# Attention step 0: first half of each tile with one wide exponential, the shift by the maximum and the sums on VectorE

## The chip, the cores and the metric

The kernel runs on one core of one Trainium2 chip. The metric is the device time of one execution in microseconds, the median of several.

## The reference, cut to what matters

A decoder block with post layer norm on x of shape (8, 512, 512), in float32:

```python
x = layernorm(x + mixing(x))               # per head: cumulative sum of FFT products, then w_out
x = layernorm(x + cross_attention(x, ctx)) # 16 heads of 32, 77 keys
x = layernorm(x + ffn(x))                  # weight rounded to int4 levels, bias, low-rank part

def cross_attention(q, c, mask):
    q, k, v = q @ W_q + b_q, c @ W_k + b_k, c @ W_v + b_v      # 16 heads
    scores = einsum('bhqd,bhkd->bhqk', q, k) / sqrt(32)
    scores = where(mask == 0, -1e6, scores)
    attn = softmax(scores, axis=-1)
    return einsum('bhqk,bhkd->bhqd', attn, v) @ W_o + b_o
```

The change touches the softmax of the first of the eight batches.

## The kernel before, in words

Three programs follow one another: `prepare` (weights, keys and values), `mix_tokens` (the mixing of all eight batches) and `attend` (cross attention and the last linear layer). Every float32 matmul is made of three: the operands are split into a high part, a rounded copy made by ScalarE, and a low part, the remainder, made by VectorE.

`attend` runs over steps. Step i holds the scores and the softmax of batch i, the turning of x1 and the projection of q of batch i + 1, and the weighing of values, the output projection and the last layer of batch i - 1. Step 0 has no batch behind it, so it has only the first two. Steps 1 to 6 share one order, steps 7 and 8 have their own.

A batch has 512 tokens, four tiles t of 128. The scores of a tile, 16 heads by 77 keys, are 1232 numbers in each partition. They lie in `score_ps`, four PSUM banks with four heads each, and one tile's scores fill it. Half h is two banks, eight heads, 616 scores. For each tile and half:

- TensorE: `score(i, t, h)`, six matmuls of 308 columns. It waits until the exponentials of the same half of the tile before have read `score_ps` (semaphore `exped`).
- VectorE: `softmax_top(i, t, h)`, which writes the masked value (`copy_predicated`, L1658) and takes the negated maximum of each head (L1663) into `top` (`topped`).
- ScalarE: `exponentials(i, t, h)`, eight instructions (L1352), one a head, with the negated maximum as bias and the sum taken by the accumulator. They write `probs`, which has room for two tiles.
- VectorE: `invert_totals(i, t)`, one reciprocal of the 16 sums (L1670).
- GpSimd: `normalize_probs(i, t, h)`, two multiplications of 616 (L1501).
- TensorE: `turn_probs(i, t, c)`, three groups of four transposes (L1146), named P{t}{c}. ScalarE copies each group (L1359) and VectorE takes its remainder (`split_probs`, L1642), which frees the bank.

Beside this TensorE turns the next batch's x1 (`turn_x1`, L1109, X0 to X3, split by L1335 and L1615) and projects q (`project_q`, Q0 to Q3, twelve matmuls of 512 columns, split by L1340 and L1623).

The P, X and Q groups share four PSUM banks, `shared_ps`, in the fixed order `START_ORDER`: P00 P01 P02 X0 X1 X2 X3 P10 P11 P12 Q0 P20 P21 Q1 P22 Q2 P30 P31 P32 Q3. Each use waits until the use four places before it has been emptied by VectorE (semaphore `freed`, counted in this order).

Every engine has its own list of calls, written out by hand. Its instructions run in that order, each held only by semaphores. Late in step 0 ScalarE also splits the two weights `w_o` and `w_ffn` (L1439, L1445), VectorE takes the remainder of `w_o` (L1825), and GpSimd that of `w_ffn`.

Of the kernel before, what the change touches and what calls it, by code (L numbers as in the profile page):

```python
# [21 lines left out]
ALU = mybir.AluOpType  # L22
ACT = mybir.ActivationFunctionType
AX = mybir.AxisListType

P = 128
B, S, D = 8, 512, 512
NT = S // P
# [3 lines left out]
XH, XHD = 16, 32  # L32
# [22 lines left out]
def wait_reuse(eng, sem, value):  # L55

    if not isinstance(value, int) or value > 0:
        eng.wait_ge(sem, value)
# [900 lines left out]
def attend(nc, ins, out, x1_dram, k_dram, v_dram, ffn_dram, ident, half_power, w_q, bias_q, bias_v, bias_o, bias_f,  # L959
# [3 lines left out]
    with ExitStack() as ctx:  # L963
# [35 lines left out]
        turned, turned_hi = sem("turned_p"), sem("pT_hi_ready")  # L999
        stat_done, stat_seen, aggr_done = sem("stat_done"), sem("stat_seen"), sem("aggr_done")  # L1000
# [101 lines left out]
        def _(pe):  # L1102
# [20 lines left out]
            def score(i, s, t, h):  # L1123

                if t == 0:

                    pe.wait_ge(k_loaded, nth(i, 1, 0) * (16 * 2 * GH))
                    pe.wait_ge(q_hi, nth(i, NC, 2 * h + 1))
                    pe.wait_ge(freed, s.emptied_before(f"Q{2 * h + 1}"))

                wait_reuse(pe, exped, i * (NT * XH) + ((t - 1) * XH + (h + 1) * XH // 2))
                tok = slice(t * P, (t + 1) * P)
                for g in (2 * h, 2 * h + 1):
                    last = split_matmuls(nc, score_ps[:, g, 0:GK],
                                         [([q[:, g, tok] for q in qT], [k[:, g, :] for k in k_block])])
                last.then_inc(scored, 1)
# [115 lines left out]
            turn_x1(1, s, 0)  # L1252
            score(0, s, 2, 1)
            turn_x1(1, s, 1)
            score(0, s, 3, 0)
# [4 lines left out]
            turn_probs(0, s, 1, 2)  # L1260
            score(0, s, 3, 1)
# [69 lines left out]
        def _(act):  # L1331
# [10 lines left out]

            def exponentials(i, t, h):

                act.wait_ge(topped, nth(i, NT * 2, 2 * t + h))
                if h == 0:

                    wait_reuse(act, turned, i * NT * 3 + (3 * (t - 1)))
                    wait_reuse(act, totalled, i * NT + (t - 1))
                for j in range(h * XH // 2, (h + 1) * XH // 2):  # L1350
                    g, k = j // GH, j % GH
                    nc.scalar.activation(probs[:, t % 2, j * KEYS:(j + 1) * KEYS],  # L1352
                                         score_ps[:, g, k * KEYS:(k + 1) * KEYS], ACT.Exp, bias=top[:, t % 2, j:j + 1],
                                         accum_out=total[:, t % 2, j:j + 1]).then_inc(exped, 1)
# [60 lines left out]
            exponentials(0, 0, 0)  # L1415
            exponentials(0, 0, 1)
            exponentials(0, 1, 0)
            exponentials(0, 1, 1)
            exponentials(0, 2, 0)
            split_probs(0, s, 0, 0)  # L1420
            split_probs(0, s, 0, 1)
            split_probs(0, s, 0, 2)
            split_x1(1, s, 0)
            exponentials(0, 2, 1)
            split_x1(1, s, 1)
# [5 lines left out]
            exponentials(0, 3, 0)  # L1431
# [177 lines left out]
        def _(dve):  # L1609
# [55 lines left out]

            def invert_totals(i, t):
# [122 lines left out]
            softmax_top(0, 0, 0)  # L1789
            softmax_top(0, 0, 1)  # L1790
            softmax_top(0, 1, 0)
            invert_totals(0, 0)
            softmax_top(0, 1, 1)
            softmax_top(0, 2, 0)
            invert_totals(0, 1)
            softmax_top(0, 2, 1)
            split_probs(0, s, 0, 0)
            split_probs(0, s, 0, 1)
            split_probs(0, s, 0, 2)
            split_x1(1, s, 0)  # L1800
            softmax_top(0, 3, 0)
            invert_totals(0, 2)
            split_x1(1, s, 1)
            split_x1(1, s, 2)
            split_x1(1, s, 3)
            softmax_top(0, 3, 1)
            split_probs(0, s, 1, 0)
            split_probs(0, s, 1, 1)
            split_probs(0, s, 1, 2)
            find_hidden(1)  # L1810
            invert_totals(0, 3)
            split_q(1, s, 0)
# [8 lines left out]

# [172 lines left out]
```

## Time and profile before

| | |
|---|---|
| median of three runs | 968.82 us |
| lowest and highest run | 965.21 and 971.74 us |
| profiled execution, first to last instruction (the page gives no other time for it) | 964.6 us |
| TensorE busy in it | 917.6 us |
| VectorE busy | 666.7 us |
| ScalarE busy | 376.8 us |
| GpSimd busy | 337.8 us |
| mean granted clock of TensorE | 0.982 |

Busy time is the union of an engine's instructions. Waiting on semaphores is not busy. The granted clock is the share of TensorE's full clock that it was given.

### The profile page before, as it was taken

The numbers are of one execution on the slowest core, as the hardware profiler recorded it, in microseconds if no ns is written. First come the engines' busy times: TensorE is split into PE (matmuls) and PEld (weight loads), VectorE is DVE, ScalarE is ACT, GpSimd is POOL, SyncE is SP. The second block draws the span as 40 slices with busy tenths as digits, with TensorE's granted clock in tenths as the row PEclk, the third lists the DMA queues.
The fourth block names the chain that finished last, engine by engine and source line by source line (L and its number), as shares of the span: only waits on it lengthen the run. The fifth ranks groups of instructions, "written<-read, shape, count | busy, mean of one in ns | idle before, by whom it ended". The sixth has DMA issues, their size and how long they took to land.

```text
span 964.6 us, 14638 instructions
## 1 busy us (share of the span) xinstructions
PE 917.6 (95%) x4476; PEld 754.5 (78%) x4476; DVE 666.7 (69%) x1128; ACT 376.8 (39%) x1403; POOL 337.8 (35%) x310
## 2 busy tenths in 40 slices
PE   5898999999999999999779999999999999999987
PEld 4784888888888888888668788888888888888775
DVE  3363466665656565555667888979889798887957
ACT  3152120101010111102287566656567565666610
POOL 2000243232222232324236434444443444433733
PEclk9998999999999999999979999999999999999999
DMA  5944201221203020203423122131222203120021
GB/s 179 326 148 172 90 1 52 80 80 52 104 28 127 3 87 1 88 23 116 134 81 102 25 79 73 40 113 24 89 63 78 75 21 122 30 89 21 17 77 44
DMA packets 72346, 76.02 MB, mean 79 GB/s; under 512 B 38567, under 2 KB 40871, under 8 KB 72303
## 3 DMA queue, kind: packets, MB, share of 16 engines
q1 hardware_dynamic: 72303, 75.49, 24.4%
q8 instruction: 22, 0.36, 0.2%
q14 instruction: 21, 0.17, 0.1%
HBM read 52.60 MB, written 22.87 MB: 78 GB/s over the span
## 4 chain that ended last, share of the span: by engine, by line
PE 41%; DVE 4%; ACT 2%; issue 2%; POOL 2%; POOLq 0%; DVEq 0%
PE shared_ps L74 31%; PE score_ps L74 4%; PE shared_ps L1146 4%; ACT probs L1352 2%; PE shared_ps L1109 1%; PE shared_ps L1179 1%; POOL probs L1501 1%; DVE score_ps L1658 1%; DVE xT_lo L1615 0%; DVE x_and_res L1704 0%; DVE top_s L1663 0%; DVE pT_lo L1642 0%; POOL x_and_res L1516 0%; DVE y L1682 0%; DVE w_o_lo L1825 0%
## 5 line engine op out<-in xcount | busy, mean ns | idle before, releaser
L1352 ACT ACTIVATE probs<-score_ps,top_s 128x77 f32<-128x77 f32 x512 | 159.0, 359 | 36.9 <-DVE top_s L1663 36.9
L1352 ACT ACTIVATION_READ_ACCUMULATOR probs<-score_ps,top_s 128x1 f32 x512 | 122.9, 240 | 0.0
L1501 POOL TENSOR_TENSOR probs<-probs,per_total 128x616 f32<-128x616 f32 x64 | 82.7, 1309 | 65.9 <-DVE per_total L1670 65.7
L1494 POOL TENSOR_TENSOR rstd<-ve,half_power 128x1 f32<-128x1 f32 x64 | 42.4, 662 | 157.1 <-DVE ve L1693 152.5
L722 POOL TENSOR_TENSOR vals<-qs_prod 128x512 f32<-128x512 f32 x32 | 41.1, 1296 | 127.1 <-DVE qs_prod L804 127.1
L713 POOL TENSOR_TENSOR mix_rstd<-mix_ve,half_power 128x1 f32<-128x1 f32 x32 | 22.0, 688 | 175.4 <-DVE mix_ve L823 175.4
L1658 DVE COPY_PREDICATED score_ps<-hidden,masked 128x616 f32<-128x616 int32 x64 | 66.2, 1034 | 11.6 <-PE score_ps L74 11.6
L1359 ACT ACTIVATE pT_hi<-shared_ps 103x512 fp32r<-103x512 f32 (+1 forms) x96 | 54.7, 612 | 46.0 <-PE shared_ps L1146 45.5
L672 ACT ACTIVATE v_sb<-v_ps 128x512 f32<-128x512 f32 x32 | 18.9, 594 | 133.9 <-PE v_ps L74 133.9
L679 ACT ACTIVATE qT_hi<-vals 128x512 fp32r<-128x512 f32 x32 | 19.4, 631 | 122.3 <-POOL vals L722 106.2
L1642 DVE TENSOR_TENSOR pT_lo<-shared_ps,pT_hi 103x512 fp32r<-103x512 f32 (+1 forms) x96 | 64.5, 684 | 0.0
L1146 PE MATMUL shared_ps<-ident,probs 128*103 128x128 f32 (+1 forms) x384 | 53.9, 279 | 2.6 <-POOL probs L1501 1.8
L74 PE MATMUL shared_ps<-w_o_hi,xT_hi 128*128 128x512 f32 x128 | 53.3, 417 | 2.3 <-DVE xT_lo L1623 1.9
L74 PE MATMUL shared_ps<-w_ffn_hi,xT_hi 128*128 128x512 f32 x120 | 50.1, 418 | 5.5 <-DVE xT_lo L1615 4.9
L1516 POOL TENSOR_TENSOR x_and_res<-x_and_res,bias_f 128x512 f32<-128x512 f32 x32 | 42.2, 1318 | 35.9 <-DVE x_and_res L1704 23.1
L1146 PEld LDWEIGHTS shared_ps<-ident,probs 128*103 128x103 f32 (+1 forms) x384 | 47.0, 158 | 9.7 <-POOL probs L1501 2.7
L1663 DVE TENSOR_REDUCE top_s<-score_ps 128x8 f32<-128x616 f32 x64 | 51.2, 800 | 3.6
L815 DVE TENSOR_TENSOR mix_r<-out_ps,x_res 128x512 f32<-128x512 f32 x29 | 20.1, 692 | 47.3 <-PE out_ps L74 47.3
L74 PE MATMUL v_ps<-xT_hi,w_spec_hi 128*128 128x512 f32 x128 | 50.6, 395 | 1.9 <-DVE xT_lo L766 1.9
L74 PE MATMUL k_ps<-xT_hi,w_spec_hi 128*128 128x512 f32 x128 | 51.7, 404 | 0.0
L74 PE MATMUL q_ps<-xT_hi,w_spec_hi 128*128 128x512 f32 x128 | 51.2, 400 | 0.0
L74 PE MATMUL shared_ps<-w_o_hi,xT_lo 128*128 128x512 f32 x128 | 50.7, 396 | 0.0
(218 smaller groups left out, 2660.1 us busy)
## 6 DMA issues: line engine op xcount, KB each, us to landing
x_tok<-in_x SPq DMA_DIRECT2D x8, 1024.0 KB, 5.9
x_res<-in_x SPq DMA_DIRECT2D x8, 1024.0 KB, 8.0
x_between<-mix_x SPq DMA_DIRECT2D x32, 256.0 KB, 2.0
x<-x_between SPq DMA_DIRECT2D x8, 1024.0 KB, 5.5
x_tok<-x_between SPq DMA_DIRECT2D x8, 1024.0 KB, 5.7
out<-y_out SPq DMA_DIRECT2D x32, 256.0 KB, 2.0
wqkv_sb<-in_w_qkv SPq DMA_DIRECT2D x4, 768.0 KB, 7.8
keys_split<-w_q_hi SPq DMA_DIRECT2D x8, 154.0 KB, 5.4
```

The source lines that it names most:

```text
L74: last = nc.tensor.matmul(out, l, r, start=(n == 0), stop=(n == len(terms) - 1))
L713: nc.gpsimd.tensor_tensor(rstd[:, t % 2:t % 2 + 1], ve[:, t % 2:t % 2 + 1], half_power[:], ALU.pow).then_inc(rstd_ready, 1)
L722: nc.gpsimd.tensor_tensor(vals[:, h, :], qs[:, 2 * h, :], qs[:, 2 * h + 1, :], ALU.subtract if h else ALU.add).then_inc(vals_summed, 1)
L1146: last = nc.tensor.transpose(shared_ps[s.bank(use)][0:size, g * P:(g + 1) * P], probs[:, t % 2, g * GK + at:g * GK + at + size], ident[:])
L1352: nc.scalar.activation(probs[:, t % 2, j * KEYS:(j + 1) * KEYS], score_ps[:, g, k * KEYS:(k + 1) * KEYS], ACT.Exp, bias=top[:, t % 2, j:j ...
L1359: nc.scalar.activation(pT[0][0:size, c, :, t * P:(t + 1) * P], turned_bank(s, t, c), ACT.Copy).then_inc(turned_hi, 1)
L1494: nc.gpsimd.tensor_tensor(rstd[:, n:n + 1], ve[:, n:n + 1], half_power[:], ALU.pow).then_inc(rstd_ready, 1)
L1501: nc.gpsimd.tensor_tensor(p, p, per_total[:, t % 2, h * heads:(h + 1) * heads].unsqueeze(2) .to_broadcast([P, heads, KEYS]), ALU.mult).the ...
L1516: nc.gpsimd.tensor_tensor(res2[:, t % 2, :], x2[:, t % 2, :], bias_f[:], ALU.add).then_inc(res2_ready, 1)
L1642: nc.vector.tensor_tensor(pT[1][0:size, c, :, tok], turned_bank(s, t, c), pT[0][0:size, c, :, tok].bitcast(F32), ALU.subtract).then_inc(fr ...
L1658: nc.vector.copy_predicated(s4, hidden[:, t, :].unsqueeze(1).unsqueeze(1).to_broadcast(shape), masked[:].unsqueeze(1).unsqueeze(1).to_broa ...
L1663: nc.vector.tensor_reduce(top[:, t % 2, h * 8:(h + 1) * 8].rearrange("p (g j) -> p g j", j=GH), s4, AX.X, ALU.max, negate=True).then_inc(t ...
```

## The change

It touches step 0 alone. For the first half of each tile, `exponentials(0, t, 0)` becomes `wide_exponential(t)`: one instruction over the 616 scores in `probs`, in place. VectorE's new `shift(t)` first adds the negated maxima to the scores and writes them to `probs`, and its new `sum_probs(t)` adds up the exponentials of each head. Two semaphores are new. TensorE's scores of the first half of the next tile wait for `shifted` and no longer for the exponentials. The second half keeps its eight exponentials.

The orders of step 0 are changed on three engines. On TensorE X1 comes ahead of score (2, 1), and score (3, 0) moves from ahead of X2 to behind P12. On ScalarE the first half of tile 2 comes behind the copies of P00 to P02, and X1's copy ahead of the second half of tile 2. On VectorE the remainders of P00 to P02 come ahead of both halves of tile 2, those of X0 and X1 ahead of the second half of tile 2, those of X2, X3 and P10 to P12 ahead of tile 3, and each inversion stands behind a sum.

```diff
--- before.py
+++ after.py
@@ -997,6 +997,7 @@
         scored, hid, topped, exped, totalled, normed = (sem("scored"), sem("hid"), sem("topped"), sem("exped"),
                                                        sem("per_total_ready"), sem("normed"))
         turned, turned_hi = sem("turned_p"), sem("pT_hi_ready")
+        shifted, summed = sem("shifted"), sem("summed")
         stat_done, stat_seen, aggr_done = sem("stat_done"), sem("stat_seen"), sem("aggr_done")
         var_eps, rstd_ready, x2_ready, y_ready = sem("var_eps_b"), sem("rstd_b"), sem("x2_ready"), sem("y_ready")
         y_stored = [sem(f"y_stored{n}") for n in range(2)]
@@ -1128,7 +1129,10 @@
                     pe.wait_ge(q_hi, nth(i, NC, 2 * h + 1))
                     pe.wait_ge(freed, s.emptied_before(f"Q{2 * h + 1}"))
 
-                wait_reuse(pe, exped, i * (NT * XH) + ((t - 1) * XH + (h + 1) * XH // 2))
+                if isinstance(i, int) and i == 0 and h == 0:
+                    wait_reuse(pe, shifted, t)
+                else:
+                    wait_reuse(pe, exped, i * (NT * XH) + ((t - 1) * XH + (h + 1) * XH // 2))
                 tok = slice(t * P, (t + 1) * P)
                 for g in (2 * h, 2 * h + 1):
                     last = split_matmuls(nc, score_ps[:, g, 0:GK],
@@ -1250,14 +1254,14 @@
             turn_probs(0, s, 0, 1)
             turn_probs(0, s, 0, 2)
             turn_x1(1, s, 0)
+            turn_x1(1, s, 1)
             score(0, s, 2, 1)
-            turn_x1(1, s, 1)
-            score(0, s, 3, 0)
             turn_x1(1, s, 2)
             turn_x1(1, s, 3)
             turn_probs(0, s, 1, 0)
             turn_probs(0, s, 1, 1)
             turn_probs(0, s, 1, 2)
+            score(0, s, 3, 0)
             score(0, s, 3, 1)
             project_q(1, s, 0)
             turn_probs(0, s, 2, 0)
@@ -1340,10 +1344,15 @@
                 nc.scalar.activation(qT[0][:, c, :], shared_ps[s.bank(use)][:], ACT.Identity,
                                      bias=bias_q[:, c:c + 1]).then_inc(q_hi, 1)
 
+            def wide_exponential(t):
+                act.wait_ge(shifted, t + 1)
+                half = probs[:, t % 2, 0:XH // 2 * KEYS]
+                nc.scalar.activation(half, half, ACT.Exp).then_inc(exped, XH // 2)
+
             def exponentials(i, t, h):
 
                 act.wait_ge(topped, nth(i, NT * 2, 2 * t + h))
-                if h == 0:
+                if h == 0 or (isinstance(i, int) and i == 0):
 
                     wait_reuse(act, turned, i * NT * 3 + (3 * (t - 1)))
                     wait_reuse(act, totalled, i * NT + (t - 1))
@@ -1412,23 +1421,23 @@
 
 
             s = Shared(0, False, True, True)
-            exponentials(0, 0, 0)
+            wide_exponential(0)
             exponentials(0, 0, 1)
-            exponentials(0, 1, 0)
+            wide_exponential(1)
             exponentials(0, 1, 1)
-            exponentials(0, 2, 0)
             split_probs(0, s, 0, 0)
             split_probs(0, s, 0, 1)
             split_probs(0, s, 0, 2)
+            wide_exponential(2)
             split_x1(1, s, 0)
+            split_x1(1, s, 1)
             exponentials(0, 2, 1)
-            split_x1(1, s, 1)
             split_x1(1, s, 2)
             split_x1(1, s, 3)
             split_probs(0, s, 1, 0)
             split_probs(0, s, 1, 1)
             split_probs(0, s, 1, 2)
-            exponentials(0, 3, 0)
+            wide_exponential(3)
             exponentials(0, 3, 1)
             split_q(1, s, 0)
             split_probs(0, s, 2, 0)
@@ -1662,6 +1671,25 @@
                 wait_reuse(dve, exped, i * NT * XH + (t - 1) * XH)
                 nc.vector.tensor_reduce(top[:, t % 2, h * 8:(h + 1) * 8].rearrange("p (g j) -> p g j", j=GH), s4, AX.X,
                                         ALU.max, negate=True).then_inc(topped, 1)
+
+            def shift(t):
+
+                dve.wait_ge(topped, 2 * t + 1)
+                wait_reuse(dve, turned, 3 * (t - 1))
+                shape = [P, GROUPS // 2, GH, KEYS]
+                s4 = score_ps[:, 0:2, 0:GK].rearrange("p g (j k) -> p g j k", j=GH)
+                low = top[:, t % 2, 0:XH // 2].rearrange("p (g j) -> p g j", j=GH).unsqueeze(3).to_broadcast(shape)
+                nc.vector.tensor_tensor(probs[:, t % 2, 0:XH // 2 * KEYS].rearrange("p (g j k) -> p g j k", j=GH, k=KEYS),
+                                        s4, low, ALU.add).then_inc(shifted, 1)
+
+            def sum_probs(t):
+
+                dve.wait_ge(exped, t * XH + XH // 2)
+                wait_reuse(dve, totalled, t - 1)
+                nc.vector.tensor_reduce(total[:, t % 2, 0:XH // 2],
+                                        probs[:, t % 2, 0:XH // 2 * KEYS].rearrange("p (j k) -> p j k", k=KEYS), AX.X,
+                                        ALU.add).then_inc(summed, 1)
+                dve.wait_ge(summed, t + 1)
 
             def invert_totals(i, t):
                 dve.wait_ge(exped, nth(i, NT * XH, t * XH + XH - 1))
@@ -1787,29 +1815,37 @@
             find_hidden(0)
             s = Shared(0, False, True, True)
             softmax_top(0, 0, 0)
+            shift(0)
             softmax_top(0, 0, 1)
             softmax_top(0, 1, 0)
+            shift(1)
+            sum_probs(0)
             invert_totals(0, 0)
             softmax_top(0, 1, 1)
-            softmax_top(0, 2, 0)
-            invert_totals(0, 1)
-            softmax_top(0, 2, 1)
             split_probs(0, s, 0, 0)
             split_probs(0, s, 0, 1)
             split_probs(0, s, 0, 2)
+            softmax_top(0, 2, 0)
+            shift(2)
+            sum_probs(1)
+            invert_totals(0, 1)
             split_x1(1, s, 0)
-            softmax_top(0, 3, 0)
-            invert_totals(0, 2)
             split_x1(1, s, 1)
+            softmax_top(0, 2, 1)
             split_x1(1, s, 2)
             split_x1(1, s, 3)
-            softmax_top(0, 3, 1)
             split_probs(0, s, 1, 0)
             split_probs(0, s, 1, 1)
             split_probs(0, s, 1, 2)
+            softmax_top(0, 3, 0)
+            shift(3)
+            sum_probs(2)
+            invert_totals(0, 2)
+            softmax_top(0, 3, 1)
             find_hidden(1)
+            split_q(1, s, 0)
+            sum_probs(3)
             invert_totals(0, 3)
-            split_q(1, s, 0)
             split_probs(0, s, 2, 0)
             split_probs(0, s, 2, 1)
             split_q(1, s, 1)
@@ -1818,7 +1854,6 @@
             split_probs(0, s, 3, 0)
             split_probs(0, s, 3, 1)
             split_probs(0, s, 3, 2)
-
             dve.wait_ge(w_hi, 1)
             dve.wait_ge(w_loaded[0], 16)
             for c in range(NC):
```

## Rows read from the trace of the kernel before

**Rows 1.** The page's first part: busy time, share of the span, instructions.

```profile
PE 917.6 (95%) x4476; PEld 754.5 (78%) x4476; DVE 666.7 (69%) x1128; ACT 376.8 (39%) x1403; POOL 337.8 (35%) x310
```

**Rows 2.** By stage: length, busy PE, PEld, DVE, ACT, POOL, clock, DMA, GB/s.

```profile
475.00:518.10 43.10, 33.42 (x162) 29.01 (x163) 28.32 (x46) 33.74 (x149) 13.58 (x11) 0.80 0.30 92
518.10:964.60 446.50, 430.14 (x2240) 360.82 (x2238) 371.15 (x665) 250.04 (x1093) 207.14 (x188) 0.99 0.22 63
```

**Rows 3.** Waits in step 0: who for whom, us in total, times, longest.

```profile
POOL probs L1501 <- DVE per_total L1670: 22.6, 4, 7.0
...
PE score_ps L74 <- ACT probs L1352: 5.5, 3, 2.9
```

**Rows 4.** TensorE's timeline in step 0: start, duration, tile, idle before.

```profile
481.83 0.41 PE L74 MATMUL score_ps<-xT_hi,qT_hi 128*128 128x308 f32 x1 [2.93 <-ACT probs L1352]
...
484.29 0.62 PE L74 MATMUL score_ps<-xT_hi,qT_hi 128*128 128x308 f32 x1 [1.08 <-ACT probs L1352]
...
487.68 0.63 PE L74 MATMUL score_ps<-xT_hi,qT_hi 128*128 128x308 f32 x1 [1.48 <-ACT probs L1352]
...
489.38 2.76 PE L1146 MATMUL shared_ps<-ident,probs 128*103 128x128 f32 x12
491.94 1.00 PE L1109 MATMUL shared_ps<-ident,x 128*128 128x128 f32 x4
...
496.25 1.11 PE L1109 MATMUL shared_ps<-ident,x 128*128 128x128 f32 x4 [2.47 <-DVE pT_lo L1642]
...
503.42 0.40 PE L74 MATMUL shared_ps<-xT_hi,w_q_hi 128*128 128x512 f32 x1
...
506.17 1.17 PE L1146 MATMUL shared_ps<-ident,probs 128*103 128x128 f32 x8
...
515.05 0.50 PE L74 MATMUL shared_ps<-xT_hi,w_q_hi 128*128 128x512 f32 x1 [0.26 <-DVE qT_lo L1623]
...
517.91 0.30 PE L74 MATMUL score_ps<-xT_hi,qT_hi 128*128 128x308 f32 x1
```

**Rows 5.** VectorE's timeline in step 0, same columns.

```profile
483.38 0.81 DVE L1658 COPY_PREDICATED score_ps<-hidden,masked 128x616 f32<-128x616 int32 x1 [2.65 <-PE score_ps L74]
484.23 0.80 DVE L1663 TENSOR_REDUCE top_s<-score_ps 128x8 f32<-128x616 f32 x1
484.94 0.24 DVE L1670 RECIPROCAL per_total<-total 128x16 f32<-128x16 f32 x1
486.38 0.81 DVE L1658 COPY_PREDICATED score_ps<-hidden,masked 128x616 f32<-128x616 int32 x1 [1.19 <-PE score_ps L74]
...
491.32 0.24 DVE L1670 RECIPROCAL per_total<-total 128x16 f32<-128x16 f32 x1
...
495.51 1.88 DVE L1642 TENSOR_TENSOR pT_lo<-shared_ps,pT_hi 103x512 fp32r<-103x512 f32 x3
...
500.65 0.24 DVE L1670 RECIPROCAL per_total<-total 128x16 f32<-128x16 f32 x1
```

**Rows 6.** ScalarE's timeline in step 0: first and ninth exponential, two copies.

```profile
479.22 0.33 ACT L1352 ACTIVATE probs<-score_ps,top_s 128x77 f32<-128x77 f32 x1 [4.90 <-DVE top_s L1663]
...
481.63 0.37 ACT L1352 ACTIVATE probs<-score_ps,top_s 128x77 f32<-128x77 f32 x1
...
500.74 0.60 ACT L1359 ACTIVATE pT_hi<-shared_ps 103x512 fp32r<-103x512 f32 x1
...
511.38 1.91 ACT L1439 ACTIVATE w_o_hi<-x_tok 128x2048 fp32r<-128x2048 f32 x1
```

**Rows 7.** VectorE's timeline in step 1: a mask.

```profile
529.47 3.75 DVE L1658 COPY_PREDICATED score_ps<-hidden,masked 128x616 f32<-128x616 int32 x1
```

**Rows 8.** GpSimd's timeline beside that mask.

```profile
530.17 2.39 POOL L1501 TENSOR_TENSOR probs<-probs,per_total 128x616 f32<-128x616 f32 x2
```

**Rows 9.** TensorE's timeline in step 1, after a wait.

```profile
543.43 0.47 PE L74 MATMUL shared_ps<-w_ffn_hi,xT_hi 128*128 128x512 f32 x1 [2.33 <-DVE xT_lo L1615]
...
547.85 1.03 PE L1146 MATMUL shared_ps<-ident,probs 128*103 128x128 f32 x8
```

## The prediction

> **What bounds the kernel now.** I read the page's busy times first. TensorE is busy 95% of the span and VectorE 69% [rows 1]. Cut by stage, the 43.1 us of attention step 0 stand out: TensorE is busy 33.4 of them, so some 9.7 us are idle, and its mean granted clock is 0.80 against 0.99 in the 446.5 us behind, in which it is busy for 430 us [rows 2]. The steps behind are bound by TensorE. So what counts is when TensorE's first score of step 1 starts, now at 517.91 [rows 4].
>
> The waits in step 0 say for whom it idles: two long ones before the scores of tile 1 and one before those of tile 2, for ScalarE's exponentials, 5.5 us in all [rows 3]; and 2.47 us before the second turn of x1, which needs the bank of a P piece that VectorE has not yet emptied [rows 4]. GpSimd waits 22.6 us for the inverted sums [rows 3]. That costs nothing now: the turns of tile 1's P start at about 500, and its sums are inverted at 491.32, those of tile 2 at 500.65 for turns at 506.17 [rows 4, 5]. The order written for VectorE keeps these slacks, and this is what the change touches.
>
> **The prices.** A mask with its maximum takes 1.56 us until VectorE's next instruction (483.38 to 484.94), and others see the maximum 0.83 after the reduction starts [rows 5]. Eight exponentials with their accumulator reads take 2.41 us (479.22 to 481.63) [rows 6]. The shift over 616 elements isn't in the trace. The nearest row is the reduction over the same 616 scores from PSUM, 0.80 us, 0.71 until the next instruction [rows 5]; three subtractions of 512 take 1.88, about 0.6 each [rows 5], so the ends are 0.6 and, if a broadcast operand ran at the mask's pace, 0.81. I take 0.72, and 0.83 for whoever depends on it. The same for the sum over 616 of SBUF, and 0.1 more before the inversion, which waits for it. The wide exponential lies between the copies of 512 (0.60) and 2048 elements (1.91): 0.85 ns an element, so 0.69 us, with 0.6 until the next [rows 6]; the low end is 0.60, the high end, if an exponential carried the 0.1 that 77-element ones (0.33) have over that line at its start, 0.79.
> A score of six matmuls takes 2.1 us until its mask starts (484.29 to 486.38) [rows 4, 5] at half clock, 1.2 of 2.4 GHz; at full clock some 0.7 less, half of the time that its matmuls take. Twelve turns of P take 2.56 at half clock (489.38 to 491.94) [rows 4]. A projection of q is 2.75 (503.42 to 506.17) [rows 4].
>
> **What is gained.** In each of four tiles ScalarE gives back 2.41 - 0.60 = 1.8 us, 7.2 in all. TensorE's scores of the next tile's first half wait for a shift and not for eight exponentials.
> Tile 0: mask at 477.5, shift at 479.2, seen at 480.05. Tile 1's first scores start there, not at 481.83 [rows 4]: 1.8 us early. But the second maximum of tile 0 now stands behind the shift and comes at 481.6; its eight exponentials run 481.6 to 484.05; before the change the ninth began at 481.63 [rows 6], and they ended at 484.03. Nothing is gained there. The second half of tile 1 waits for them: 484.15, against 484.29 [rows 4]. Its eight exponentials end at 490.4 as before.
> Tile 2's first scores follow at once, at 485.9 (before: 487.68 [rows 4]), and the first turn of P waits for GpSimd instead: shift, sum and inversion of tile 1 and 0 stand in VectorE's queue, so tile 0 is inverted at 485.4 (before 484.94 [rows 5]), normalized in 3 us to 488.7, turned from 488.8 (before 489.38 [rows 4]). X0, X1, score 2/1, X2 and X3 then run without a wait, since VectorE now empties the banks from 491.0 and not from 495.51 [rows 5]. TensorE is through with them at 495.2; before, they ended at about 500. Up to here the change is 4.8 us ahead, and the 2.47 us wait is gone.
>
> **What is lost.** VectorE now does the three remainders of tile 0's P (491.0 to 493.1) ahead of the mask of tile 2. Then mask and maximum (to 494.8), shift (495.5), sum of tile 1 (496.2), inversion at 496.3. Before it was 491.32 [rows 5]: 5.0 us later. GpSimd normalizes from 496.7 in 2.39 [rows 8] and tile 1 can be turned at 499.2. TensorE, done at 495.2, waits 4.0 us: the lead is lost to the first new wait, on tile 1's sums.
> Beside it, ScalarE's wide exponential of tile 2 waits for its shift until 495.6, and ahead of x1's copies, which end at 497.2. VectorE's remainders of X0 and X1 are ahead of mask 2/1: 498.1, maximum 499.7, exponentials to 502.1, only then X2's copy and remainder, 503.4. The last turn of tile 1 needs X2's bank: 503.5, a second wait, 2.5 us. Behind it come score 3/0 (504.5), 3/1 and the first projection of q, at 507.6 in half clock, at 505.7 in full; before, 503.42 [rows 4].
> Tile 3's first mask waits for score 3/0: 506.5. Maximum, shift and the sum of tile 2 follow, and tile 2 is inverted at 509.7, against 500.65 [rows 5]: 9 us later. Normalized at 512.4, turned at 512.6, against 506.17 [rows 4]: 6.4 us late, a third wait of 2.2 us behind the first projection. Tile 3's sum waits for nothing that matters: inverted at 516.2, normalized at 518.9, turned from 521.4.
>
> **The clock.** After the wait of 2.33 us in step 1 the twelve matmuls of 512 columns take 4.42 us (543.43 to 547.85), where 2.75 is the rate at full clock [rows 4, 9]: 1.7 us more. The third new wait meets the same work, two turns and a projection, so I add 1.7. From 512.6: turns and Q1 to 518.2, P22 and Q2 to 521.4, tile 3's turns to 522.7, 0.4 more for Q2's bank, and the last projection at 523.1. It was at 515.05 [rows 4]: 8.1 us late. Walking the old order with the same prices puts it at 515.6, 0.6 too late, so I take 7.5.
>
> **What follows the stage.** The splitting of w_o and w_ffn, the last q's and bias additions all hang on the same late events and move along. TensorE has 16 us idle in the 446.5 behind [rows 2], spread and at the end, so little can be made up. Sum: +7.5 us. No transfer is moved. The profiled execution would go from 964.6 to 972.1. The page gives only its span; the median of the three runs is 4.2 us above it, and they spread by 6.5. So 968.8 + 7.5 = 976.3.
>
> **The rivals.**
> *The shorter chain pays through.* If VectorE's queue did not hold back the second halves and sums, two exponential groups on the way to tile 2 would shrink from 2.41 to 0.72: 3.4 us, 965.4, faster than before. For it: exponentials are what TensorE waits for now [rows 3]. It decides at the turns of tile 1: it holds if they start before 496. Against it: their sums stand behind seven VectorE instructions, of which the first wait for ScalarE's copies. 6%.
> *Clock or step 1 gives back.* At full clock all through the walk ends 4.9 us late; or the 2.33 us wait of step 1, with its 1.7 of slow clock, closes in a shifted order, 7.5 - 4.0 = 3.5. About 973. 20%.
> *Collisions on top.* A mask in step 1 took 3.75 us where 0.81 is usual: it lasted until GpSimd had finished two multiplications, 530.17 to 532.56 [rows 5, 7, 8]. Now mask 2/1 (498.1) falls into GpSimd's work on tile 1 (496.7 to 499.1), on the path: up to 1 us. Mask 3/1 meets tile 2's: 0.6 to 2.4. With half clock held longer behind the third wait, 1 to 2 more: 3 in the middle, up to 6, so 979 to 982, over 1% slower. 25%.
> The Trainium skill, SBUF — State Buffer, "Who interferes with whom", says that a VectorE instruction with two SBUF inputs and a GpSimd one that reads SBUF hold the shared pair exclusively, and whoever starts first blocks the other. By that rule mask 2/1 waits whole, as the row of 529.47 shows; without it this rival would lose most of its chance.
> *It does not do what it says:* shift or sum at twice the price. Two shifts and two sums on the path: up to +3 beside the above; or everything is hidden, 0. 4%.
> The forecast itself, +5.5 to +9.5: 45%.
>
> **How the numbers follow.** Likeliest: 976.3. 1% is 9.7 us, about what a measurement can tell. Over it lie most of the collisions and an edge of the forecast with the scatter of medians: 0.27. Faster by over 1% needs three times the rival's gain: 0.03. Range: from just above the first rival, 967, to the heavy end with 2 us of scatter, 984.
>
> **What would show it.** Tile 1's first scores near 480.1; no wait before X1; TensorE idle 4 us before tile 1's turns, released by GpSimd, 2.5 before its last turn, released by VectorE's X2, and about 2 before tile 2's, by GpSimd; inversions near 485.4, 496.3, 509.7 and 516.2; step 1's first score near 525.5. Wrong is the prediction if tile 2 is inverted before 505, if TensorE never waits for GpSimd, or if the end moves otherwise than step 1's start.

## The result, and the profile after

The median went from 967.13 us (965.21 to 971.74, four runs) to 975.99 us (974.07 to 978.69, four runs), 8.9 us more: a ratio of 1.0093, 95% interval 1.0058 to 1.0127. The median of before that the prediction had in hand, 968.82, was that of three of these runs.

The profiled executions differ by more, 964.6 against 975.9 us. 1.8 us of this had arisen before step 0: its first score starts at 477.38 and not at 475.58, in code that is the same. In all the profiles of this study, of kernels that are the same up to there, it starts between 474.7 and 477.9. So times within step 0 are given below less 1.8, or from the first score on.

TensorE's timeline of the changed kernel, with the idle time before an instruction and its releaser in brackets:

```profile
477.38 0.38 PE L74 MATMUL score_ps<-xT_hi,qT_hi 128*128 128x308 f32 x1 [1.99 <-PEq L457]
...
482.73 0.41 PE L74 MATMUL score_ps<-xT_hi,qT_hi 128*128 128x308 f32 x1 [3.42 <-DVE probs L1682]
...
486.87 0.62 PE L74 MATMUL score_ps<-xT_hi,qT_hi 128*128 128x308 f32 x1 [2.67 <-ACT probs L1361]
...
490.92 1.56 PE L1150 MATMUL shared_ps<-ident,probs 128*103 128x128 f32 x12 [0.65 <-POOL probs L1510]
...
494.50 0.66 PE L1110 MATMUL shared_ps<-ident,x 128*128 128x128 f32 x4 [1.58 <-DVE pT_lo L1651]
...
501.53 2.03 PE L1150 MATMUL shared_ps<-ident,probs 128*103 128x128 f32 x8 [4.65 <-POOL probs L1510]
506.83 1.09 PE L1150 MATMUL shared_ps<-ident,probs 128*102 128x128 f32 x4 [3.27 <-DVE xT_lo L1624]
...
510.71 0.40 PE L74 MATMUL shared_ps<-xT_hi,w_q_hi 128*128 128x512 f32 x1
...
516.18 1.12 PE L1150 MATMUL shared_ps<-ident,probs 128*103 128x128 f32 x8 [2.57 <-POOL probs L1510]
517.06 0.48 PE L74 MATMUL shared_ps<-xT_hi,w_q_hi 128*128 128x512 f32 x1
...
521.48 0.60 PE L1150 MATMUL shared_ps<-ident,probs 128*102 128x128 f32 x4
...
529.27 0.30 PE L74 MATMUL score_ps<-xT_hi,qT_hi 128*128 128x308 f32 x1
```

Compare with [rows 4]. From the first score of step 0 to that of step 1 it is 51.9 us, where it was 42.3: 9.6 more. Behind it are 446.6 and 446.7 us, so nothing was given back and nothing lost. Three waits are new or have grown: 4.65 us before the turns of tile 1, released by GpSimd, 3.27 before its last turn, released by VectorE's remainders of x1 (0.89 at this place before), and 2.57 before the turns of tile 2, by GpSimd again. The projection behind the third runs at half clock for most of its length: 517.06 to 521.48, 4.42 us.

VectorE's timeline, the lines that answer to [rows 5] and the new ones:

```profile
477.44 2.62 DVE L1658 TENSOR_SCALAR hidden<-mask 128x308 int32<-128x308 int32 x1
480.19 0.81 DVE L1667 COPY_PREDICATED score_ps<-hidden,masked 128x616 f32<-128x616 int32 x1
...
481.87 0.80 DVE L1682 TENSOR_TENSOR probs<-score_ps,top_s 128x616 f32<-128x616 f32 x1
...
486.77 0.78 DVE L1689 TENSOR_REDUCE total<-probs 128x8 f32<-128x616 f32 x1
487.58 0.25 DVE L1698 RECIPROCAL per_total<-total 128x16 f32<-128x16 f32 x1
...
498.75 0.25 DVE L1698 RECIPROCAL per_total<-total 128x16 f32<-128x16 f32 x1
...
500.55 1.59 DVE L1667 COPY_PREDICATED score_ps<-hidden,masked 128x616 f32<-128x616 int32 x1
...
512.86 0.25 DVE L1698 RECIPROCAL per_total<-total 128x16 f32<-128x16 f32 x1
...
519.34 0.25 DVE L1698 RECIPROCAL per_total<-total 128x16 f32<-128x16 f32 x1
```

The shift takes 0.80 us and the sum 0.78. The second inversion is at 498.75 and the third at 512.86, against 491.32 and 500.65 [rows 5]. The mask at 500.55 lasts 1.59 us, and the table of hidden keys at 477.44 lasts 2.62. The wide exponential on ScalarE:

```profile
482.76 0.72 ACT L1350 ACTIVATE probs<-probs 128x616 f32<-128x616 f32 x1 [6.64 <-DVE probs L1682]
```

GpSimd's normalization of tiles 1 and 2:

```profile
499.09 2.39 POOL L1510 TENSOR_TENSOR probs<-probs,per_total 128x616 f32<-128x616 f32 x2 [8.22 <-DVE per_total L1698]
513.19 2.94 POOL L1510 TENSOR_TENSOR probs<-probs,per_total 128x616 f32<-128x616 f32 x2 [11.71 <-DVE per_total L1698]
```

The waits of step 0, for whom, in total, times, longest:

```profile
POOL probs L1510 <- DVE per_total L1698: 31.5, 4, 11.7
...
PE shared_ps L1150 <- POOL probs L1510: 7.9, 3, 4.6
```

GpSimd waits 31.5 us for the inverted sums, where it was 22.6 [rows 3], and TensorE now waits 7.9 us for GpSimd, where it did not wait at all. The 5.5 us for the exponentials of [rows 3] have become 3.42 for the first shift and 2.67 for exponentials.

Event by event, the changed kernel's times less 1.8:

| event | before | forecast | measured |
|---|---|---|---|
| first scores of tile 1 | 481.83 | 480.05 | 480.9 |
| tile 0 inverted | 484.94 | 485.4 | 485.8 |
| turns of tile 0 | 489.38 | 488.8 | 489.1 |
| tile 1 inverted | 491.32 | 496.3 | 496.9 |
| turns of tile 1 | about 500 | 499.2 | 499.7 |
| last turn of tile 1 | | 503.5 | 505.0 |
| first projection | 503.42 | 507.6 | 508.9 |
| tile 2 inverted | 500.65 | 509.7 | 511.1 |
| turns of tile 2 | 506.17 | 512.6 | 514.4 |
| last projection | 515.05 | 523.1 | 524.6 |
| first score of step 1 | 517.91 | 525.5 | 527.5 |

### The profile page after: what moved, and what is told of

The parts are those of the page before. It is cut to its first block, busy times and chain, and to the rows that moved or that the text cites. A ratio compares the mean times of both kernels' runs of the same rounds, so it can differ in the third digit from the quotient of the medians.

```text
span 975.9 us, 14596 instructions
## 1 busy us (share of the span) xinstructions
PE 918.2 (94%) x4476; PEld 754.6 (77%) x4476; DVE 675.0 (69%) x1136; ACT 368.9 (38%) x1343; POOL 337.8 (35%) x310
## 3 DMA queue, kind: packets, MB, share of 16 engines
q1 hardware_dynamic: 72303, 75.49, 24.2%
## 4 chain that ended last, share of the span: by engine, by line
PE 40%; DVE 4%; issue 3%; ACT 2%; POOL 2%; POOLq 0%; DVEq 0%; ACTq 0%
PE shared_ps L74 30%; PE score_ps L74 4%; PE shared_ps L1150 3%; ACT probs L1361 2%; POOL probs L1510 1%; DVE score_ps L1667 1%; PE shared_ps L1110 1%; PE shared_ps L1183 1%; DVE top_s L1672 1%; DVE xT_lo L1624 0%; DVE x_and_res L1732 0%; DVE pT_lo L1651 0%; DVE hidden L1658 0%; POOL x_and_res L1525 0%; DVE y L1710 0%
## 5 line engine op out<-in xcount | busy, mean ns | idle before, releaser
L1361 ACT ACTIVATE probs<-score_ps,top_s 128x77 f32<-128x77 f32 x480 | 148.9, 356 | 38.1 <-DVE top_s L1672 38.1
L1361 ACT ACTIVATION_READ_ACCUMULATOR probs<-score_ps,top_s 128x1 f32 x480 | 114.6, 239 | 0.0
L74 PE MATMUL v_ps<-xT_hi,w_spec_lo 128*128 128x512 f32 x128 | 51.3, 401 | 0.0
L74 PE MATMUL v_ps<-xT_lo,w_spec_hi 128*128 128x512 f32 x128 | 51.2, 400 | 0.0
```

What stands on the lines that cost most here:

```text
L74: last = nc.tensor.matmul(out, l, r, start=(n == 0), stop=(n == len(terms) - 1))
```

## The experiments

The theory: the orders cost the time, not the added arithmetic. The sums of tiles 1 and 2 stand behind remainders that wait for others, and X2's bank hangs on the late second half of tile 2. The main rival: VectorE's eight added instructions, four shifts and four sums. Each kernel is compared with runs of the kernel before on the same chip, whose medians were 966.2 to 966.8 us. "Stage" is the time from the first score of step 0 to the first value matmul of step 1 in the profiled execution: 43.2 us before, 52.7 in the changed kernel. "Rest" is what follows: 445.9 and 445.8. Both are of one execution each. A projection can run at half clock in one and at full clock in another at the same place, which is worth 1.6 us (the rows are below, under the remainder of w_o and under the clearings), so a smaller difference of stage or rest is no finding by itself.

### The two halves of the change apart

`o1_orders_alone` has the changed kernel's orders and the arithmetic of before. Against the changed kernel, for each tile like this:

```diff
-            wide_exponential(0)
+            exponentials(0, 0, 0)
...
             softmax_top(0, 0, 0)
-            shift(0)
...
-            sum_probs(0)
             invert_totals(0, 0)
```

`a1_arith_alone` has the changed kernel's arithmetic in the orders of before: each shift right behind its half's maximum and each sum right ahead of its inversion, but for the shift of tile 3. Against the kernel before, on VectorE:

```diff
             softmax_top(0, 3, 0)
+            sum_probs(2)
             invert_totals(0, 2)
             split_x1(1, s, 1)
             split_x1(1, s, 2)
             split_x1(1, s, 3)
+            shift(3)
             softmax_top(0, 3, 1)
```

> The arithmetic of before (eight exponentials with accumulators in the first half too, no shift, no sum), in the orders of the changed kernel on TensorE, ScalarE and VectorE. Theory (the orders cost the time): the sums of tile 1 and of tile 2 still stand behind the remainders of the tile before, so TensorE waits at the turns of tile 1 and of tile 2 and before the last turn of tile 1; walked with the prices of the rows, step 0 ends 6.0 us later than before, about 973. Rival (the twelve-odd VectorE instructions that were added cost the time): the time of before, 967 within 1.

> The wide exponential, the shift and the sum, in the orders of before; the shift of tile 3 has to stand right ahead of the maximum of tile 3's second half, since it waits for tile 1's last turn. Theory (orders): most of the loss is gone, the walk ends 2.4 us later than before (the shift of tile 2 waits for the turns of tile 0 and holds VectorE), about 969.5. Rival (load on VectorE): 975 or more. Rival (the shorter chain pays through where the orders don't hold it): 964.

Orders alone: 973.38 us, ratio 1.0083 (1.0065 to 1.0100), stage 50.3. Arithmetic alone: 966.59 us, ratio 1.0005 (0.9992 to 1.0019). So the orders carry 7 to 8 of the 8.9 us, and the eight VectorE instructions (the expectation says twelve, miscounted) and the wide exponentials, in the orders of before, neither cost nor gain. TensorE's timeline of the first:

```profile
499.33 2.01 PE L1146 MATMUL shared_ps<-ident,probs 128*103 128x128 f32 x8 [4.36 <-DVE xT_lo L1615]
505.19 1.10 PE L1146 MATMUL shared_ps<-ident,probs 128*102 128x128 f32 x4 [3.86 <-DVE xT_lo L1615]
...
512.88 1.12 PE L1146 MATMUL shared_ps<-ident,probs 128*103 128x128 f32 x8 [1.01 <-POOL probs L1501]
```

TensorE waits at the same three places without any shift or sum. But the first wait, before tile 1's turns, is released here by a remainder of x1 and not by GpSimd, the third is 1.01 us and not 2.57, and the projection behind it ran at full clock (2.84 us). In the arithmetic-alone kernel the profiled stage was 45.2 us, 2.0 above before, as the walk had it (2.4), while its median shows no difference; that execution was the slowest of its ten, and its table of hidden keys took 2.63 us.

### Taking the new waits away one by one

`c1_sum1_early`, against the changed kernel, on VectorE:

```diff
             softmax_top(0, 1, 1)
+            sum_probs(1)
+            invert_totals(0, 1)
             split_probs(0, s, 0, 0)
...
             shift(2)
-            sum_probs(1)
-            invert_totals(0, 1)
```

`c3_both` has this too, and the following on VectorE, and on ScalarE the same with `exponentials(0, 2, 1)` in the place of `softmax_top(0, 2, 1)`:

```diff
             split_x1(1, s, 1)
-            softmax_top(0, 2, 1)
             split_x1(1, s, 2)
             split_x1(1, s, 3)
+            softmax_top(0, 2, 1)
```

> The changed kernel with the sum and the inversion of tile 1 moved ahead of the remainders of tile 0's P on VectorE, and nothing else. Theory (the three waits stand in a row, each hides behind the next): tile 1 is normalized some 5 us earlier and TensorE starts its turns then, but the last of them still needs X2's bank, which hangs on the late second half of tile 2; the wait moves there and the time stays that of the changed kernel, within 1.5 us. Rival (the first wait is paid by itself): its 4.65 us come off, and 971 or less.

> The same and also X2's and X3's copies and remainders ahead of the second half of tile 2 on ScalarE and VectorE, so that both of the first two new waits are taken away. Theory: the maximum of tile 2's second half comes later still, TensorE's last scores wait for it, and the sums of tile 2 stay late behind tile 3's mask and shift; the wait before tile 2's turns grows to about 3 us and only 0.7 us comes off, 975. Rival (the first two waits are the cost): 4.65 and 3.27 us come off, 968.

976.96 us, ratio 1.0093 (1.0057 to 1.0129), and 977.17 us, ratio 1.0101 (1.0074 to 1.0129): neither differs from the changed kernel. TensorE's timeline of the first of them:

```profile
501.80 2.01 PE L1150 MATMUL shared_ps<-ident,probs 128*103 128x128 f32 x8 [3.68 <-DVE xT_lo L1624]
507.66 1.10 PE L1150 MATMUL shared_ps<-ident,probs 128*102 128x128 f32 x4 [3.86 <-DVE xT_lo L1624]
...
517.03 1.12 PE L1150 MATMUL shared_ps<-ident,probs 128*103 128x128 f32 x8 [2.69 <-POOL probs L1510]
```

and of the second:

```profile
499.81 2.85 PE L1150 MATMUL shared_ps<-ident,probs 128*103 128x128 f32 x12 [3.68 <-DVE xT_lo L1624]
...
505.66 0.41 PE L74 MATMUL score_ps<-xT_hi,qT_hi 128*128 128x308 f32 x1 [1.95 <-ACT probs L1361]
...
514.47 2.03 PE L1150 MATMUL shared_ps<-ident,probs 128*103 128x128 f32 x8 [3.37 <-POOL probs L1510]
```

In the first, tile 1 is inverted at 494.57 instead of 498.75, and still TensorE starts the same turns 24.1 us behind its first score (24.2 in the changed kernel). It waits 3.68 us for a remainder of x1, since that remainder starts at 500.96, where it was 499.35, and X1's wait has grown from 1.58 to 3.18. So the expectation was right on the time and wrong on the way: the turns did not start earlier. What follows waits 3.86 and 2.69. In the second the turns start 23.2 us behind the first score and the wait before the last turn is gone, and a wait of 1.95 for the second half's exponentials and one of 3.37 before tile 2's turns stand in its place. The waits lie behind one another on VectorE's queue: taking the first away, or the first two, moves the loss and leaves the sum, so neither is the cost by itself. The third was not taken away alone.

### The same arithmetic in another order

`w1_wide_new_order` is an order sought with the prices of the prediction, on all three engines. VectorE's list, where it matters, against the changed kernel:

```diff
             invert_totals(0, 0)
+            sum_probs(1)
             softmax_top(0, 1, 1)
+            softmax_top(0, 2, 0)
+            shift(2)
+            invert_totals(0, 1)
             split_probs(0, s, 0, 0)
             split_probs(0, s, 0, 1)
             split_probs(0, s, 0, 2)
-            softmax_top(0, 2, 0)
-            shift(2)
-            sum_probs(1)
-            invert_totals(0, 1)
+            softmax_top(0, 2, 1)
             split_x1(1, s, 0)
+            sum_probs(2)
             split_x1(1, s, 1)
-            softmax_top(0, 2, 1)
             split_x1(1, s, 2)
             split_x1(1, s, 3)
+            invert_totals(0, 2)
+            softmax_top(0, 3, 0)
+            shift(3)
...
```

The remainder of w_o, four instructions, also moves from behind P32's remainder to ahead of P30's, and ScalarE's copy of w_o to behind P12's. On ScalarE the second halves of tiles 2 and 3 also move back, behind x1's copies and behind P21's, and on TensorE score (2, 1) comes ahead of X0 and score (3, 0) ahead of P11.

`n1_narrow_same_order` is this order with the arithmetic of before, `n2_narrow_own_order` an order sought for that arithmetic.

> The arithmetic of the changed kernel (same instructions, same number) in another order: VectorE masks and shifts tile 2 and inverts tile 1 ahead of the remainders of tile 0, sums and inverts tile 2 ahead of tile 3's mask, and ScalarE copies all of x1 ahead of the second half of tile 2. Theory (orders): the three waits of TensorE for sums and for X2 go, the walk ends 5 us ahead of before and 12 ahead of the changed kernel, about 963. Rival (load on VectorE, or the half clock, costs the time whatever the order): not under 971.

> The eight narrow exponentials in the orders of w1_wide_new_order, without shift and sums. Theory (order and arithmetic both count: the new order lives on the 1.8 us that ScalarE gives back in each tile and on scores that wait for a shift): the walk ends where the kernel before ends, 967 within 1.5. Rival (it was the order alone): 959 to 961 like the wide one.

> The arithmetic of before in an order made for it: inversion of tile 1 ahead of the remainders of tile 0, tile 0's first turn ahead of tile 2's scores, the exponentials of tiles 2 and 3 behind copies. Theory: the walk ends 3.6 us ahead of before, about 963, so a part of the gain of w1_wide_new_order was there without the wide exponential, and 3 to 4 us of it need it. Rival (the order of before was the best for its arithmetic): 966 or more.

| kernel | median us | ratio to before | stage us | rest us |
|---|---|---|---|---|
| w1_wide_new_order | 959.01 | 0.9940 (0.9917 to 0.9962) | 40.3 | 441.5 |
| n1_narrow_same_order | 962.43 | 0.9961 (0.9947 to 0.9975) | 43.9 | 441.0 |
| n2_narrow_own_order | 963.39 | 0.9970 (0.9956 to 0.9985) | 41.3 | 443.5 |

With the very instructions of the changed kernel, the first is 1.5% under it and 0.6% under before. TensorE's timeline:

```profile
490.83 0.41 PE L74 MATMUL score_ps<-xT_hi,qT_hi 128*128 128x308 f32 x1 [1.78 <-ACT probs L1361]
...
495.77 0.66 PE L1150 MATMUL shared_ps<-ident,probs 128*103 128x128 f32 x4 [0.42 <-DVE xT_lo L1624]
...
510.45 1.56 PE L1150 MATMUL shared_ps<-ident,probs 128*103 128x128 f32 x12 [1.25 <-POOL probs L1510]
```

One short wait for GpSimd is left (1.25), before tile 3's turns. Two things came out otherwise than expected. The stage fell by 2.9 us, as against 5 expected, and the rest by 4.4, which wasn't expected. And n1, walked at the time of before, has the stage of before within 0.7, as the walk said, but is 4.8 us faster in the rest. n2 met its number, 963, with half of its reason: 3.6 us were expected of the stage, which gave 1.9, and the rest gave 2.4. So the wide exponential is worth 3.6 us of the profiled stage in this order; some 1.7 of it is a slower clock in n1, behind a wait of 2.33 us before tile 3's turns. By the medians it is 3.4 (959.01 against 962.43, on different chips), by the ratios 2.0, with intervals that overlap. The gain in the rest is common to both.

### Where the gain behind step 0 comes from

The kernels with the new order have the remainder of w_o ahead of tile 3's remainders. In the kernel before, that work and what it meets, VectorE's and GpSimd's timelines:

```profile
516.70 2.49 DVE L1825 TENSOR_TENSOR w_o_lo<-x_tok,w_o_hi 128x512 fp32r<-128x512 f32 x4
```

```profile
517.56 7.67 POOL L1560 TENSOR_TENSOR w_ffn_lo<-x_and_res,w_ffn_hi 128x512 fp32r<-128x512 f32 x4 [6.52 <-ACT w_ffn_hi L1445]
```

`t1_before_wo_first` moves this alone in the kernel before, `t2_after_wo_first` in the changed one:

```diff
-            split_probs(0, s, 3, 0)
-            split_probs(0, s, 3, 1)
-            split_probs(0, s, 3, 2)
             dve.wait_ge(w_hi, 1)
             dve.wait_ge(w_loaded[0], 16)
             for c in range(NC):
                 nc.vector.tensor_tensor(w_o[1][:, c, :], raw_o[:, c, :], w_o[0][:, c, :].bitcast(F32),
                                         ALU.subtract).then_inc(w_o_lo, 1)
+            split_probs(0, s, 3, 0)
+            split_probs(0, s, 3, 1)
+            split_probs(0, s, 3, 2)
             split_q(1, s, 3)
```

> The kernel before, with one thing moved: VectorE takes the remainder of w_o (four instructions with two SBUF inputs) ahead of tile 3's three remainders and not behind them. Theory (n1_narrow_same_order has the stage length of before and is 4 us faster: what it gains lies in step 1, and comes from this move): GpSimd's remainder of w_ffn no longer meets it and takes 5.6 us instead of 7.67, its later work ends earlier against TensorE, the blocked mask of step 1 falls from 3.75 to about 2.5, and TensorE's wait before the first projection with w_ffn, 2.33 us with a slow clock behind it, falls under 1.5 and keeps its clock: 963, 3 to 4 us under before. Rival (something else of the new order did it): 966 to 967.

> The changed kernel with the same move. Theory: the gain behind step 0 is independent of the loss in it, so 3 to 4 us come off here too, 972. Rival (the change's late sums already moved GpSimd's work): 975 to 976.

962.02 us, ratio 0.9965 (0.9948 to 0.9981), and 973.27 us, ratio 1.0072 (1.0056 to 1.0088), against 1.0093 for the changed kernel. GpSimd in the first:

```profile
517.19 5.59 POOL L1560 TENSOR_TENSOR w_ffn_lo<-x_and_res,w_ffn_hi 128x512 fp32r<-128x512 f32 x4 [6.54 <-ACT w_ffn_hi L1445]
```

VectorE:

```profile
514.54 2.49 DVE L1821 TENSOR_TENSOR w_o_lo<-x_tok,w_o_hi 128x512 fp32r<-128x512 f32 x4
...
529.72 1.66 DVE L1658 COPY_PREDICATED score_ps<-hidden,masked 128x616 f32<-128x616 int32 x1
```

and TensorE, before the first projection with w_ffn:

```profile
541.76 0.48 PE L74 MATMUL shared_ps<-w_ffn_hi,xT_hi 128*128 128x512 f32 x1 [0.57 <-DVE xT_lo L1615]
...
544.63 1.03 PE L1146 MATMUL shared_ps<-ident,probs 128*103 128x128 f32 x8
```

The two remainders no longer overlap. GpSimd's takes 5.59 us instead of 7.67, the blocked mask 1.66 instead of 3.75 [rows 7], TensorE's wait is 0.57 us and not 2.33, and its projection takes 2.87 (541.76 to 544.63) and not 4.42 [rows 9]. The stage is 43.8 us, 0.6 over before, and the rest 440.7 instead of 445.9.

Not all of these 5.2 us are the chain just told. From the first value matmul to the end of that projection it is 25.7 us where it was 29.1, 3.4 less. The other 1.8 lie near the end of the kernel, in twelve matmuls of 512 columns behind a wait, in code that the move doesn't touch. In the kernel before and in t1:

```profile
932.86 0.59 PE L74 MATMUL shared_ps<-w_o_hi,xT_hi 128*128 128x512 f32 x1 [1.86 <-DVE xT_lo L1623]
...
937.28 0.39 PE L74 MATMUL shared_ps<-w_o_hi,xT_hi 128*128 128x512 f32 x1
```

```profile
929.42 0.47 PE L74 MATMUL shared_ps<-w_o_hi,xT_hi 128*128 128x512 f32 x1 [1.77 <-DVE xT_lo L1623]
...
932.23 0.39 PE L74 MATMUL shared_ps<-w_o_hi,xT_hi 128*128 128x512 f32 x1
```

They take 4.42 and 2.81 us. It is 2.82 in `o1_orders_alone`, which doesn't have the move, and 4.36 to 4.42 in the seven other profiles without it; n1, t2, w1 and w2 have the fast one and n2 the slow one. Whether the move has a part in this, no run decides. One move of four instructions gives 3.4 us by the ratio, 4.7 by the medians. In the changed kernel the profiled rest fell alike, to 440.6; its medians and ratio speak for 2 to 3 us, with intervals that overlap widely.

### The clearings of the value blocks

On GpSimd, in the changed kernel (`m1_memset_later`), the kernel before (`t3_before_memset_later`) and the best one (`w2_wide_memset_later`):

```diff
+            pool.wait_ge(hidden_ready, 1)
             for tile in v_block:
```

> The changed kernel, with GpSimd's two clearings of the value blocks held until VectorE has made the hidden table of batch 0. In the changed kernel's trace that table took 2.62 us beside both clearings, in the trace of before 1.30 beside one. Theory: it is an exclusive block, a matter of phase and no part of the change; the table takes 0.3, its mask starts when the first scores are there, and the time falls by 0.9 us against the changed kernel, some 975. Rival (the block costs nothing, the scores decide): the same as the changed kernel.

> The kernel before with GpSimd's clearings held until the hidden table is made. Theory: the table takes 0.3 us instead of 1.30 or 2.62, the first mask starts with the first scores, and TensorE's chain over the first two tiles with it; 1 to 2 us under before, 965, with a smaller spread between runs. Rival (the first scores decide): the same.

> w1_wide_new_order with the clearings held too. Theory: 0.5 to 1.5 us under w1_wide_new_order, 958. Rival: the same, 959, or above it where the clearings end later.

The table of hidden keys took 0.32 us in all three (row of the first, VectorE):

```profile
474.78 0.32 DVE L1659 TENSOR_SCALAR hidden<-mask 128x308 int32<-128x308 int32 x1
```

| kernel | median us | ratio to before |
|---|---|---|
| m1_memset_later | 972.65 | 1.0079 (1.0057 to 1.0100) |
| t3_before_memset_later | 965.79 | 0.9998 (0.9986 to 1.0009) |
| w2_wide_memset_later | 959.45 | 0.9931 (0.9913 to 0.9948) |

In the kernel before it is worth nothing: its profiled stage is the same 43.2 us with the table at 1.30 or 0.32, so the 1 to 2 us expected were wrong. In the changed kernel the stage of the profiled execution was 50.5 us at 0.32, 51.3 at 1.30 (in `t2_after_wo_first`), and 52.7 at 2.62. There the first shift stands right behind the table and releases tile 1's scores, but most of the difference has another reason. Up to tile 2's turns the three are 38.2, 38.4 and 38.8 us behind the first score: 0.6 for the table. The projection behind them is the rest. In m1:

```profile
512.93 1.12 PE L1150 MATMUL shared_ps<-ident,probs 128*103 128x128 f32 x8 [1.98 <-POOL probs L1510]
513.80 0.48 PE L74 MATMUL shared_ps<-xT_hi,w_q_hi 128*128 128x512 f32 x1
...
516.64 0.60 PE L1150 MATMUL shared_ps<-ident,probs 128*102 128x128 f32 x4
```

It takes 2.84 us behind a wait of 1.98, and 2.87 in t2 behind one of 2.21, where the changed kernel's took 4.42 behind 2.57. The ratio of m1 is lower than the changed kernel's, with overlapping intervals, so in the median this stays open. w2 is not told apart from w1. Both beat the two kernels of the comparison.

## Why the prediction was right

Forecast 976.3 us and +7.5; measured 975.99 and +8.9 (profiled stage +9.6). The shift and its mechanism were right. That the time was met within 0.3 us is luck: the median before that it was added to, of three runs, lay 1.7 us above that of the four, and the shift was 1.4 too small.

- **The gains, 4.8 us ahead until X3.** Tile 1's first scores came 0.9 us early, not 1.8; the scores of its second half, behind the exponentials, came 0.8 later than before, where 0.1 earlier was forecast. One statement was wrong: X1 did wait, 1.58 us, since the twelve turns ran at full clock (1.56 us, 2.56 forecast) and VectorE's remainders of P came 0.95 later than forecast. It cost nothing: TensorE was through with X3 at 495.1, 495.2 forecast, and waited for tile 1's sums anyway.
- **First new wait, tile 1's sums.** 4.0 us forecast, 4.65 measured, the turns at the forecast time within 0.5. That it was not the cost by itself, which the prediction left unsaid, is what the kernels without it show: without it the same turns still started 24.1 and 23.2 us behind the first score, against 24.2, held by a remainder of x1.
- **Second, X2's bank.** 2.5 forecast, 3.27 measured. The mask of tile 2's second half fell into GpSimd's normalization and took 1.59 us, 0.8 more than usual: the collision that the third rival had priced at up to 1 us, at its place.
- **Third, tile 2's sums.** 2.2 forecast, 2.57 measured. The inversion came 10.4 us later than before (9 forecast), and the normalization took 2.94 instead of 2.39, with the mask of tile 3's second half inside it.
- **The clock.** 1.7 us forecast for the projection behind the third wait, 4.42 - 2.75 = 1.67 measured in this execution (1.56 against the 2.86 that the same projection took before). It is no sure term: m1 and t2 have the same orders and waits of 1.98 and 2.21 at this place, and their projections ran at full clock.
- **Shift, sum, wide exponential.** 0.72 to 0.83, the same, and 0.69 forecast; 0.80, 0.78 and 0.72 measured.
- **What was missed.** 0.85 us at the start, where the table of hidden keys was blocked for 2.62 us and held the first mask: mis-sized at zero. The stage fell 2.0 us short, and the event table shows where. At tile 1's turns the forecast was 0.5 short, with what was left of the late start in it; behind the first collision (0.8) it was 1.5 short, and at the last projection still 1.5, with the second collision (0.5) in it and some of the later prices too high. The last 0.5 is the deduction from 8.1 to 7.5, made because the walk of the old order came out 0.6 too late. It didn't hold for the new one.
- **Step 1.** The whole shift passed on, and the rest stayed within 0.1 us, with its own wait of 2.32. The second rival's give-back did not happen in this execution. Its two halves were seen apart: t1 and t2 close the wait by one moved block, which the prediction had not seen as a cause, and m1 keeps the wait, 2.35 us, and has the projection behind it at 2.87 us.
- **The shorter chain pays through.** It did not in these orders. In another order the profiled stage is 3.6 us shorter with it, 1.7 of them by the clock, and the medians 2 to 3.4; the first rival had worked out 3.4. The ratios' intervals, 0.9917 to 0.9962 with it and 0.9947 to 0.9975 without, don't part them.

The Trainium skill, SBUF — State Buffer, "Who interferes with whom", has VectorE with two SBUF inputs and GpSimd reading SBUF block each other. The traces agree: the mask that starts at 500.55 in the changed kernel ends at 502.14, and GpSimd's pair of normalizations ends at 501.48, so 0.66 of its 0.8 us of work came after them; and the two remainders take GpSimd 7.67 us together and 5.59 apart.

## What to carry to other kernels

In these queues written by hand the places of the instructions cost 7 to 8 us and the added instructions nothing that could be measured. Walk every queue from release to release before you move anything, and look at which waits stand in a row, since taking the first one away only shows the next. Where an engine's slack hides late sums, write down how much slack there is, and spend it knowingly. Compare one profile with another place by place before you read a difference of their lengths: here a projection that ran at half clock in one execution and not in the other was 1.6 us. Look for long instructions of VectorE and GpSimd that overlap without need; setting two of them apart gave more than half of what the best new order did.

## What the runs showed of the hardware

- VectorE's table of hidden keys, one input of 308 elements, took 0.32, 1.30 or 2.62 us: it waited for none, one or both of GpSimd's clearings of some 1.4 us each, which only write. Whether it met one or both differed between profiles of kernels whose code is the same up to there, and so it may be a part of the scatter of a kernel in which something hangs on it; that is not shown.
- VectorE's w_o remainder, which started first, kept its 2.49 us whether it met GpSimd's or not; GpSimd's gave way, by 2.1 us.
- After 2.57 us of idle TensorE ran the next eight turns and one matmul at full clock, then some eight matmuls at half (0.43 us apart where 0.23 is usual), then full again; after 1.24 us, in `w1_wide_new_order`, its projection took 2.87 and no half clock was seen. The length of the wait alone doesn't decide it: in step 1 the projection took 4.42 us behind 2.33 in the kernel before and 2.87 behind 2.35 in `m1_memset_later`, and near the end 4.41 behind 1.76 in `a1_arith_alone` and 2.80 behind 1.76 in w1.
